# Two attentions rebuilt: heads on halves of a query tile, maxima in paired banks 21 steps ahead, the mask in f32r, row sums inverted inside

## The chip, the core and the metric

The kernel runs on one core of a Trainium2 chip. The metric is the device time of one launch in microseconds (us), the median over the runs shown. The core has TensorE (matrix products into the memory PSUM, eight banks of 512 columns), VectorE, ScalarE, GpSimd and SyncE, which here issues the DMA transfers; each takes its instructions in order and waits on semaphores for the others.

## The reference, cut to what matters

The input x has 2048 rows of 512 columns. The program is a layer of attention plus a gated feed-forward layer, then a gated cumulative sum plus a second attention. The change touches the two attentions:

```python
# attention 0: 32 heads of 16, 8 key heads, causal over N = 2048
scores = einsum('bhqd,bhkd->bhqk', q, k) / sqrt(16)
weight = softmax(where(causal, scores, -inf), axis=-1)
out = einsum('bhqk,bhkd->bhqd', weight, v) @ wo
# attention 1: 16 heads of 32, the same form, causal over 2048
```

All 2048 positions are one sequence in both, so each head has 136 blocks of 128 x 128 on or under the diagonal.

## The kernel before, in words

P is 128, a chunk (CH) is 512 positions, TPC = 4 tiles make a chunk, and there are NCH = 4 chunks and QT = 16 tiles. Products run in f32r with operands split in a high and a low part. For the scores, the parts are stacked along the rows of the array: 3 * DH rows, 48 for attention 0 and 96 for attention 1, and two more rows (96 and 97) carry minus the row maximum, high and low, against ones in k. The rows between are zero in attention 0.

The heads are worked through in 8 groups, of HG = 4 heads in attention 0 and 2 in attention 1. Each group is computed twice. **Maxima** (`max_scores`, L613): TensorE multiplies one query tile i with a chunk kc of keys into a bank of `ps_1` (three banks); VectorE takes the maximum of each row into `mx_part`, with TENSOR_REDUCE (L710) for full blocks, and for blocks at the diagonal with a custom operation that adds `band` first (L706), followed by a short read of the accumulator. When all maxima of 12 tiles (early) or the last 4 (late) are there, `flip` transposes them by a matmul (L624), VectorE splits them in `take_rows` (L727, L729), and SP writes them to memory and reads them into rows 96 and 97 of q (`put_rows`, L534 and L537). **Scores with softmax**: for each chunk c of queries and key tile t (`PASS2_STEPS`, 40 steps a group, 24 full and 16 at the diagonal), TensorE computes two heads into one of two double banks `ps_s` (L663), with a bf16 matmul that adds the mask at the diagonal (L668); ScalarE takes the exponential of both heads at once into `ex` (L596); `times_v` (L635) multiplies the previous step's `ex` with v, whose ones column gives the row sums. Four heads (32 columns each) or two (64) go to column strips of the array and run side by side. At the end of a chunk VectorE copies `ps_o` out (L735) and SP stores it (L544).

The order is written out by hand: in `slot`, each step of group g also does the HG maxima matmuls of the same step of group g + 1, spread between the scores. Before the first group there is an opening with the maxima of all its 40 steps; the last group has none beside it. Three sets of q, k and v rotate; at the start of a group SP loads the set of the group after next (L512 to L521), 2.2 MB in attention 0 and 4 MB in attention 1. `over_slots` loops over three groups by a register. `reciprocals` (L965 to L973) is a block of its own behind each attention: it reads the row sums of all heads from memory, inverts them and writes them to z; `project_out` multiplies with them.

## Time and profile before

| | us |
|---|---|
| median of 3 runs (3016.12 to 3024.72) | 3019.53 |
| the profiled execution | 3012.14 |
| its span, first to last instruction | 3010.3 |
| TensorE busy (matmuls) | 2623.4 (87%) |
| VectorE busy | 1634.4 (54%) |
| ScalarE busy | 1100.0 (37%) |

The times come from one profiled execution. A busy time is the union of an engine's instructions, and matmuls are pipelined: the duration of one counts until its result is out, though the next starts earlier. How long a matmul keeps the array is read from the distance of two starts. [...] "idle before" is how long an engine had nothing to run before a group's instructions, and what ended that.

### The profile page before, as it was taken

The page shows a single profiled execution, that of the slowest core. Times are in us where ns is not written, and L with a number is a line of the kernel's source. Part 1 is how long each engine was busy: PE and PEld are TensorE (multiplying, and loading weights), DVE is VectorE, ACT ScalarE, POOL GpSimd, SP SyncE. Part 2 cuts the span into 40 slices and gives each one's busy share as a digit, 9 for nine tenths or more (in the row PEclk, how much of TensorE's full clock was granted, in tenths as well). Part 3 has the DMA queues.
Part 4 walks back from the last instruction along what each step waited for, and adds up shares of the span by engine and source line. Part 5 has one row for each costly group of instructions (what it writes and reads, how often), then busy time and mean ns, then how long its engine had stood idle before and what let it go on. Part 6 is the DMA issues. An engine that isn't in the chain of part 4 may idle for free. (4 is left out here: it accounts for less than half of the span.)

```text
span 3010.3 us, 38749 instructions
## 1 busy us (share of the span) xinstructions
PE 2623.4 (87%) x12386; PEld 1552.7 (52%) x12386; DVE 1634.4 (54%) x3332; ACT 1100.0 (37%) x1303; POOL 128.9 (4%) x84
## 2 busy tenths in 40 slices
PE   6969999589999999999995799797189999999945
PEld 3758888345555555555543577675144444444314
DVE  4644445587777777777712434311176665666313
ACT  2422222005565555555672222121014444444420
POOL 1200000300000000000000022100300000000000
PEclk8979999659999999999997899898569999999978
DMA  4741010401202202020003100252542122220023
GB/s 157 239 145 42 28 42 0 60 15 28 40 10 42 39 15 42 13 38 10 9 15 132 60 1 0 76 136 102 139 97 55 45 52 72 71 71 12 15 72 120
DMA packets 103924, 177.62 MB, mean 59 GB/s; under 512 B 39664, under 2 KB 45552, under 8 KB 97712
## 3 DMA queue, kind: packets, MB, share of 16 engines
q1 hardware_dynamic: 100272, 162.58, 20.7%
q10 hardware_dynamic: 3456, 12.58, 1.3%
q8 instruction: 104, 1.70, 0.2%
q14 instruction: 92, 0.75, 0.1%
HBM read 115.24 MB, written 59.90 MB: 58 GB/s over the span
## 5 line engine op out<-in xcount | busy, mean ns | idle before, releaser
L596 ACT ACTIVATE a_ex<-a_ps_s 128x1024 f32<-128x1024 f32 x960 | 832.6, 894 | 804.5 <-PE a_ps_s L668 404.1
L710 DVE TENSOR_REDUCE a_mx_part<-a_ps 128x1 f32<-128x512 f32 x1152 | 771.9, 688 | 255.0 <-PE a_ps L613 246.5
L613 PE MATMUL a_ps<-a_k,a_q 96*128 96x512 f32 (+3 forms) x1920 | 786.6, 452 | 97.4 <-DMA a_q<-q 92.8
L613 PEld LDWEIGHTS a_ps<-a_k,a_q 96*128 96x128 f32 x1920 | 369.5, 204 | 586.2 <-DVE a_mx_part L710 326.9
L635 PE MATMUL a_ps_o<-a_ex,a_v 128*32 128x512 f32 (+7 forms) x3840 | 607.6, 548 | 22.8 <-DVE a_o L735 19.1
L663 PE MATMUL a_ps_s<-a_q,a_k 128*128 128x512 f32 (+3 forms) x1920 | 607.6, 392 | 22.3 <-DMA a_q<-m_early 13.7
L706 DVE CUSTOM_DVE_ANT_0 a_junk<-a_ps,band 128x128 f32<-128x128 f32 (+3 forms) x768 | 369.3, 486 | 213.7 <-PE a_ps L613 210.5
L663 PEld LDWEIGHTS a_ps_s<-a_q,a_k 128*128 128x128 f32 x1920 | 353.4, 194 | 119.3 <-ACT a_ex L596 45.4
L635 PEld LDWEIGHTS a_ps_o<-a_ex,a_v 128*32 128x32 f32 (+1 forms) x3840 | 114.2, 117 | 212.9 <-issue 161.0
L668 PE MATMUL a_ps_s<-block_band,block_ident 128*128 128x128 bf16 x768 | 175.0, 234 | 0.0
L110 PE MATMUL w_ps<-w_oh,w_wh 128*128 128x512 f32 x128 | 54.7, 427 | 103.3 <-DVE w_ol L1042 103.3
L668 PEld LDWEIGHTS a_ps_s<-block_band,block_ident 128*128 128x128 bf16 x768 | 75.1, 98 | 84.7 <-issue 53.9
L110 PE MATMUL gc_bank<-xh,gc_wh 128*128 128x512 f32 x256 | 104.0, 406 | 16.3 <-DVE xl L100 16.3
L735 DVE COPY a_o<-a_ps_o 128x512 f32<-128x512 f32 x64 | 43.9, 686 | 135.6 <-PE a_ps_o L635 135.6
L939 DVE TENSOR_TENSOR mlp_hid<-mlp_ps_g,mlp_act_up 128x512 f32<-128x512 f32 x64 | 44.2, 690 | 133.2 <-PE mlp_ps_g L853 124.3
L852 PE MATMUL mlp_ps_u<-xh,mlp_w 128*128 128x512 f32 x256 | 101.2, 395 | 17.0 <-DVE mlp_w L917 17.0
L864 PE MATMUL mlp_ps_y<-mlp_hh,mlp_w 128*128 128x512 f32 x256 | 102.1, 399 | 1.5 <-DVE mlp_hl L942 1.5
L890 ACT ACTIVATE mlp_act_up<-mlp_ps_u,mlp_s 128x512 f32<-128x512 f32 x64 | 44.1, 689 | 159.2 <-PE mlp_ps_u L853 159.2
L111 PE MATMUL gc_bank<-xl,gc_wh 128*128 128x512 f32 x256 | 102.0, 399 | 0.0
L112 PE MATMUL gc_bank<-xh,gc_wl 128*128 128x512 f32 x256 | 102.0, 398 | 0.0
L1370 DVE TENSOR_TENSOR p_ol<-p_bank,p_oh 128x512 fp32r<-128x512 f32 x32 | 22.1, 692 | 145.2 <-ACT p_oh L1331 145.2
L853 PE MATMUL mlp_ps_u<-xl,mlp_w 128*128 128x512 f32 x256 | 100.9, 394 | 0.0
(161 smaller groups left out, 2536.1 us busy)
## 6 DMA issues: line engine op xcount, KB each, us to landing
a_q<-q SPq DMA_DIRECT2D x48, 512.0 KB, 12.3
o<-a_o SPq DMA_DIRECT2D x64, 256.0 KB, 2.4
q<-p_oh SPq DMA_DIRECT2D x32, 256.0 KB
q<-p_ol SPq DMA_DIRECT2D x32, 256.0 KB
w_o<-o SPq DMA_DIRECT2D x32, 256.0 KB
w_z<-z SPq DMA_DIRECT2D x32, 256.0 KB
v<-p_v SPq DMA_DIRECT2D x32, 256.0 KB, 3.4
a_k<-k SPq DMA_DIRECT2D x8, 1024.0 KB, 8.4
```

Source lines behind the costliest of these rows:

```text
L110: pe.matmul(out, wh(k), xh(k), start=k == 0, stop=False)
L111: pe.matmul(out, wh(k), xl(k), start=False, stop=False)
L112: mm = pe.matmul(out, wl(k), xh(k), start=False, stop=k == KT - 1)
L596: act.activation(ex[unit % NE][:, :, off:CH], ps_s[unit % 2][:, :, off:CH], ACT.Exp, scale=SCALE).then_inc(exp_done, 1)
L613: pe.matmul(ps_1[bank][:, 0:w], q_st[set_][0:96, h, i * P:(i + 1) * P], k_st[set_][0:96, h % KH, kc * CH:kc * CH + w], start=True, stop=True)\
L635: mm = pe.matmul(ps_o[h * CT:h * CT + VW, off:CH], v_st[set_][:, h % VH, t, :], ex[(n * PAIRS + h // 2) % NE][:, h % 2, off:CH], start=t = ...
L663: mm = pe.matmul(ps_s[unit % 2][:, h, off:CH], k_st[set_][:, (2 * pair + h) % KH, t * P:(t + 1) * P], q_st[set_][:, 2 * pair + h, c * CH + ...
L668: mm = pe.matmul(ps_s[unit % 2][:, h, off:off + P], block_ident[:, :], block_band[:, :], start=False, stop=True)
L706: dve.tensor_tensor_reduce(out=junk[b][:, 0:w], in0=bank, in1=band[:, CH - w:CH], scale=1.0, scalar=NEG, op0=ALU.add, op1=ALU.max, accum_o ...
L710: dve.tensor_reduce(out, bank, AX.X, ALU.max).then_inc(taken1, 1)
L852: pe.matmul(bank[n % 2][:, :], w[b][i][:, k, cols], xh[:, k, chunk(c)], start=k == 0, stop=False)
L864: pe.matmul(ps_y[:, m, :], w[b][2][:, e, cols], hh[n % 2][:, :], start=e == 0, stop=False)
```

## The change

Both attentions are written anew, with the same mathematics.

- `HALVES` is 2 in attention 0: q holds two heads one above the other, even ones from row 0 and odd ones from row 64 on, and k is loaded twice, into both halves. A score matmul uses 48 (maxima) or 50 rows of one half. The two rows for the maxima stand right behind the operand (row KC), so no rows need to be zero, and q is no longer cleared. Attention 1 has one half (96 and 98 rows).
- Maxima go in blocks of two heads into one of two double banks `ps_1`. VectorE takes full blocks of both heads with one TENSOR_REDUCE; diagonal ones stay one operation per head. They lead the scores by `LEAD` = 21 steps and run on through all groups, without slots. The maxima are transposed per chunk (four times a group), two steps after its last block.
- Scores go head by head into three single banks `ps_s`, with one exponential per head, and `ex` has six buffers for four. ScalarE also copies `ps_o` out.
- The mask is a product in f32r: one matmul per head in attention 1, two of 64 columns in attention 0.
- The row sums are handled inside: after the store of a chunk SP reads the row of sums back (`load_sums`), VectorE inverts it (`invert`), SP stores it (`store_sums`). The block `reciprocals` is gone.
- Loops over registers are gone: the program is written out. The first block of the program, which makes the constants, has more of them to make, by selects one after another, two DMAs and four casts.

```diff
-ATTN0 = dict(HG=4, KH=1, VH=1, DH=16, VW=32, SCALE=16 ** -0.5, GROUPS=8)
-ATTN1 = dict(HG=2, KH=2, VH=2, DH=32, VW=64, SCALE=32 ** -0.5, GROUPS=8)
+ATTN0 = dict(HG=4, KH=1, VH=1, DH=16, VW=32, SCALE=16 ** -0.5, GROUPS=8, HALVES=2)
+ATTN1 = dict(HG=2, KH=2, VH=2, DH=32, VW=64, SCALE=32 ** -0.5, GROUPS=8, HALVES=1)
...
+LEAD = 21
...
+    BLOCKS = [(g, i, kc, p) for g in range(GROUPS) for i in range(QT) for kc in range(i // TPC + 1) for p in range(PAIRS)]
+    LAST_BLOCK = {(g, i // TPC): n for n, (g, i, kc, p) in enumerate(BLOCKS)}
+    FLIP_DELAY = 2 * PAIRS
+    FLIP_AT = {n + 1 + FLIP_DELAY: f for f, n in enumerate(sorted(LAST_BLOCK.values()))}
+    STEP_LIST = [(g, c, t) for g in range(GROUPS) for c, t in PASS2_STEPS]
+    SLOTS = {s: range((s + LEAD) * PAIRS, (s + LEAD + 1) * PAIRS) for s in range(len(STEP_LIST))}
+    SLOTS[-1] = range(0, LEAD * PAIRS)
+    LAST_STEP = {s: (g, c) for s, (g, c, t) in enumerate(STEP_LIST) if t == TPC * c + TPC - 1}
...
-        ps_s = [psum(f"ps_s{i}", [P, 2, CH]) for i in range(2)]
...
+        ps_1 = [psum(f"ps_1{i}", [P, 2, CH]) for i in range(2)]
+        ps_s = [psum(f"ps_s{i}", [P, CH]) for i in range(3)]
...
+                for e in range(HALVES):
+                    r0 = e * ROWS
+                    q_half = q_heads.rearrange("(p e) s r n -> e s r p n", e=HALVES)[e]
+                    sp.dma_start(k_st[s][r0:r0 + 2 * DH].bitcast(F32), k_heads.rearrange("h s r n -> (s r) h n"))\
+                        .then_inc(landed[s], 16)
+                    for r in (0, DH):
+                        sp.dma_start(q_st[s][r0 + r:r0 + r + DH].bitcast(F32), q_half[0]).then_inc(landed[s], 16)
+                    sp.dma_start(k_st[s][r0 + 2 * DH:r0 + KC].bitcast(F32), k_heads[:, 0].rearrange("h r n -> r h n"))\
+                        .then_inc(landed[s], 16)
+                    sp.dma_start(q_st[s][r0 + 2 * DH:r0 + KC].bitcast(F32), q_half[1]).then_inc(landed[s], 16)
...
+            def load_sums(g, c):
+                j = g * NCH + c
+                b = j % 2
+                sp.wait_ge(stored[b], 16 * (j // 2 + 1))
+                if j >= 2:
+                    sp.wait_ge(inverse, j - 1)
+                src = o_d[g].rearrange("(h r) (c m n) -> c r h m n", h=HG, c=NCH, n=ZN)[c, CT // 2]
+                sp.dma_start(z[b][:, :], src).then_inc(z_in[b], 16)
...
+            for s in range(-1, len(STEP_LIST) + 8):
+                for n in SLOTS.get(s, ()):
+                    if n in FLIP_AT:
+                        put_rows(FLIP_AT[n], n)
+                if s >= 0 and s < len(STEP_LIST) and s % STEPS == 2 and s // STEPS + 2 < GROUPS:
+                    if s // STEPS > 0:
+                        sp.wait_ge(pv_done, s // STEPS * STEPS)
+                    elif ONES0 < KC:
+                        sp.wait_ge(blank, 3)
+                    load(s // STEPS + 2)
+                if s - 2 in LAST_STEP:
+                    store(*LAST_STEP[s - 2])
+                if s - 3 in LAST_STEP:
+                    load_sums(*LAST_STEP[s - 3])
+                if s - 6 in LAST_STEP:
+                    store_sums(*LAST_STEP[s - 6])
...
+            for s, (g, c, t) in enumerate(STEP_LIST):
+                if s - 2 in LAST_STEP:
+                    stage(*LAST_STEP[s - 2], s - 2)
+                off = first_col(c, t)
+                for h in range(HG):
+                    n = s * HG + h
+                    unit = s * PAIRS + h // 2
+                    act.wait_ge(scores2, n + 1)
+                    if h % 2 == 0 and unit >= NE:
+                        act.wait_ge(pv_done, (unit - NE) // PAIRS + 1)
+                    act.activation(ex[unit % NE][:, h % 2, off:CH], ps_s[n % 3][:, off:CH], ACT.Exp, scale=SCALE)\
+                        .then_inc(exp_done, 1)
...
+            def max_scores(n):
+                g, i, kc, p = BLOCKS[n]
+                s = g % NS
+                m = entry(n)
                 w = min(CH, (i + 1) * P - kc * CH)
...
+                if (i, kc, p) == (0, 0, 0):
+                    pe.wait_ge(landed[s], LOADS * (g // NS + 1))
+                if m >= 2:
+                    pe.wait_ge(taken1, m - 1)
+                for e in (1, 0):
+                    h = 2 * p + e
+                    r0, slot_h = h % HALVES * ROWS, h // HALVES
+                    mm = pe.matmul(ps_1[m % 2][:, e, 0:w], q_st[s][r0:r0 + KC, slot_h, i * P:(i + 1) * P],
+                                   k_st[s][r0:r0 + KC, h % KH, kc * CH:kc * CH + w], start=True, stop=True)
+                mm.then_inc(scores1, 1)
...
+            def scores(s, h):
+                g, c, t = STEP_LIST[s]
+                n, st = s * HG + h, g % NS
                 off = first_col(c, t)
...
+                r0, slot_h = h % HALVES * ROWS, h // HALVES
+                if n >= 3:
+                    pe.wait_ge(exp_done, n - 2)
+                diagonal = t >= TPC * c
+                mm = pe.matmul(ps_s[n % 3][:, off:CH], k_st[st][r0:r0 + KM, h % KH, t * P:(t + 1) * P],
+                               q_st[st][r0:r0 + KM, slot_h, c * CH + off:(c + 1) * CH], start=True, stop=not diagonal)
+                for part in range(HALVES if diagonal else 0):
+                    sel, low = mask
+                    cols = slice(off + part * ROWS, off + (part + 1) * ROWS)
+                    r0 = h % HALVES * ROWS
+                    mm = pe.matmul(ps_s[n % 3][:, cols], sel[r0:r0 + ROWS, part, :], low[r0:r0 + ROWS, :],
+                                   start=False, stop=part == HALVES - 1)
+                mm.then_inc(scores2, 1)
...
+            for s, (g, c, t) in enumerate(STEP_LIST):
+                if t == 0:
+                    f = g * NCH + c
+                    pe.wait_ge(rows_in[f % 2], ROWS_IN * (f // 2 + 1))
+                for p in range(PAIRS):
+                    n = SLOTS[s][p]
+                    scores(s, 2 * p)
+                    if n in FLIP_AT:
+                        flip(n)
+                    if n < len(BLOCKS):
+                        max_scores(n)
+                    scores(s, 2 * p + 1)
+                if s > 0:
+                    times_v(s - 1)
...
+                if kc < i // TPC:
+                    dve.tensor_reduce(mx_part[:, 2 * p:2 * p + 2, i, kc], bank[:, :, 0:w], AX.X, ALU.max)\
+                        .then_inc(taken1, 1)
+                    return
+                for e in range(2):
+                    last = dve.tensor_tensor_reduce(out=junk[m % 2][:, e, 0:w], in0=bank[:, e, 0:w], in1=band[:, CH - w:CH],
+                                                    scale=1.0, scalar=NEG, op0=ALU.add, op1=ALU.max,
+                                                    accum_out=mx_part[:, 2 * p + e, i, kc:kc + 1])
+                last.then_inc(taken1, 1)
...
+            def invert(g, c):
+                j = g * NCH + c
+                dve.wait_ge(z_in[j % 2], 16 * (j // 2 + 1))
+                if j >= 2:
+                    dve.wait_ge(z_out[j % 2], 16 * (j // 2))
+                dve.reciprocal(zr[j % 2][:, :], z[j % 2][:, :]).then_inc(inverse, 1)
+            for s in range(-1, len(STEP_LIST) + 8):
+                for n in SLOTS.get(s, ()):
+                    if n in FLIP_AT:
+                        take_rows(n)
+                    if n < len(BLOCKS):
+                        maxima(n)
+                        g, i, kc, p = BLOCKS[n]
+                        if LAST_BLOCK[g, i // TPC] == n:
+                            whole_max(g, i // TPC, n)
+                if s - 5 in LAST_STEP:
+                    invert(*LAST_STEP[s - 5])
...
-def reciprocals(nc, keep, sems, name, heads, rows, o_d, z_d):
...
-        block_ident, block_band = sb("block_ident", [P, P], BF16), sb("block_band", [P, P], BF16)
...
+        masks = {1: (sb("mask_sel1", [P, 1, P], F32R), sb("mask_low1", [P, P], F32R)),
+                 2: (sb("mask_sel2", [P, 2, P], F32R), sb("mask_low2", [P, P // 2], F32R))}
...
```

How the instructions move is shown at two places. The first is TensorE in attention 0 in a step with full blocks (L613 and L612 are the maxima, L663 and L633 the scores, L635 and L651 the product with v). Before:

```order
L661 REGISTER_ALU
L663 MATMUL a_ps_s<-a_q,a_k 128x512 [waits attn_exp_done]
L663 MATMUL a_ps_s<-a_q,a_k 128x512
L612 REGISTER_ALU
L613 MATMUL a_ps<-a_k,a_q 128x512 [waits attn_taken1]
L661 REGISTER_ALU
L663 MATMUL a_ps_s<-a_q,a_k 128x512 [waits attn_exp_done]
L663 MATMUL a_ps_s<-a_q,a_k 128x512
L612 REGISTER_ALU
L613 MATMUL a_ps<-a_k,a_q 128x384 [waits attn_taken1]
L635 MATMUL a_ps_o<-a_ex,a_v 32x512 [waits attn_exp_done]
L635 MATMUL a_ps_o<-a_ex,a_v 32x512 x3
```

and now:

```order
L633 MATMUL a_ps_s<-a_q,a_k 128x512 [waits at_exp_done]
L612 MATMUL a_ps<-a_k,a_q 128x512 [waits at_taken1]
L612 MATMUL a_ps<-a_k,a_q 128x512
L633 MATMUL a_ps_s<-a_q,a_k 128x512 [waits at_exp_done] x2
L612 MATMUL a_ps<-a_k,a_q 128x512 [waits at_taken1]
L612 MATMUL a_ps<-a_k,a_q 128x512
L633 MATMUL a_ps_s<-a_q,a_k 128x512 [waits at_exp_done]
L651 MATMUL a_ps_o<-a_ex,a_v 32x512 [waits at_exp_done]
L651 MATMUL a_ps_o<-a_ex,a_v 32x512 x3
```

The numbers of columns stay, eight score matmuls between two products; the pairs of maxima wait once, the scores each for a bank of their own, and successive matmuls are in opposite halves of the array.

The second is the start of a group, steps 1 to 5, on SP in attention 0 (L522 stores the last chunk of the group before, L494 to L501 load a later group, L532 reads the row sums, L509 and L514 move the maxima):

```order
L522 DMA o<-a_o 128x512 [waits at_staged]
L494 DMA a_k<-k 32x2048 [waits at_pv_done]
L497 DMA a_q<-q 16x2x2048 x2
L498 DMA a_k<-k 16x2048
L500 DMA a_q<-q 16x2x2048
L494 DMA a_k<-k 32x2048
L497 DMA a_q<-q 16x2x2048 x2
L498 DMA a_k<-k 16x2048
L500 DMA a_q<-q 16x2x2048
L501 DMA a_v<-v 128x512
L532 DMA a_z<-o 128x1x16 [waits at_inverse,at_stored1]
L509 DMA m<-a_rows_0 16x128 [waits at_taken1]
L509 DMA m<-a_rows_1 16x128
L514 DMA a_q<-m 2x2x512 [waits at_rows_out0]
```

The read of the row sums is issued behind all loads of a group; before, only the rows of maxima were there. On VectorE the inversion of them (L724) stands between the maxima (L690 and L694):

```order
L690 TENSOR_REDUCE a_mx_part<-a_ps 128x2 [waits at_scores1] x4
L724 RECIPROCAL a_zr<-a_z 128x16 [waits at_z_in0]
L690 TENSOR_REDUCE a_mx_part<-a_ps 128x2 [waits at_scores1] x2
L694 ISA a_junk,a_mx_part<-a_ps,band 128x256 [waits at_scores1]
L694 ISA a_mx_part 128x1
L694 ISA a_junk,a_mx_part<-a_ps,band 128x256
L694 ISA a_mx_part 128x1
L694 ISA a_junk,a_mx_part<-a_ps,band 128x256 [waits at_scores1]
```

Before, no instruction of VectorE in an attention waited for the row sums.

## Rows read from the trace of the kernel before

**Rows 1.** Busy time by stretch: us; PE, PEld, DVE, ACT, POOL busy (instructions); PEclk; DMA share, GB/s

```profile
574.50:672.90 98.40, 88.28 (x163) 45.08 (x163) 87.79 (x228) 0.00 (x0) 0.75 (x1) 0.50 0.19 25
680.00:1514.00 834.00, 824.40 (x4950) 437.66 (x4950) 648.25 (x1628) 480.00 (x561) 0.00 (x0) 0.99 0.15 26
1514.00:1598.00 84.00, 81.71 (x532) 33.54 (x530) 3.32 (x6) 64.97 (x78) 0.00 (x0) 1.00 0.03 11
2174.50:2233.30 58.80, 47.67 (x93) 24.64 (x93) 44.88 (x120) 1.20 (x2) 10.06 (x3) 0.50 0.40 90
2233.30:2822.60 589.30, 569.00 (x2492) 246.71 (x2491) 364.15 (x850) 251.28 (x282) 0.00 (x0) 0.99 0.22 55
2822.60:2885.00 62.40, 61.13 (x266) 21.91 (x266) 3.19 (x6) 34.62 (x39) 0.00 (x0) 1.00 0.05 18
```

**Rows 2.** Timeline of TensorE over one step: start us, us, engine, line, what, count

```profile
1139.26 1.07 PE L635 MATMUL a_ps_o<-a_ex,a_v 128*32 128x512 f32 x8
1140.26 0.68 PE L613 MATMUL a_ps<-a_k,a_q 96*128 96x512 f32 x2
1140.77 0.64 PE L663 MATMUL a_ps_s<-a_q,a_k 128*128 128x512 f32 x2
...
1141.48 0.63 PE L663 MATMUL a_ps_s<-a_q,a_k 128*128 128x512 f32 x2
1141.94 0.40 PE L613 MATMUL a_ps<-a_k,a_q 96*128 96x512 f32 x1
1142.27 0.64 PE L635 MATMUL a_ps_o<-a_ex,a_v 128*32 128x512 f32 x4
```

**Rows 3.** VectorE: group in 680:1514, timeline, the tile w_z, group of the page

```profile
L710 DVE TENSOR_REDUCE a_mx_part<-a_ps 128x1 f32<-128x512 f32 x672 | 448.8, 687 | 141.1 <-PE a_ps L613 138.0 <-issue 1.1
...
1139.13 1.29 DVE L710 TENSOR_REDUCE a_mx_part<-a_ps 128x1 f32<-128x512 f32 x2
...
L1040 DVE TENSOR_TENSOR w_o<-w_o,w_z x8: 2284/2291/2293, 1626.3 to 2984.3; 128x2048 f32<-128x2048 f32 x8
...
L706 DVE CUSTOM_DVE_ANT_0 a_junk<-a_ps,band 128x128 f32<-128x128 f32 (+3 forms) x768 | 369.3, 486 | 213.7 <-PE a_ps L613 210.5
```

**Rows 4.** ScalarE: timeline in the last group of attention 0, groups in 680:1514

```profile
1547.70 1.94 ACT L596 ACTIVATE a_ex<-a_ps_s 128x1024 f32<-128x1024 f32 x2 [0.18 <-PE a_ps_s L663]
...
L596 ACT ACTIVATE a_ex<-a_ps_s 128x1024 f32<-128x1024 f32 x392 | 380.0, 1021 | 219.8 <-PE a_ps_s L663 179.7 <-PE a_ps_s L668 39.8
...
L596 ACT ACTIVATE a_ex<-a_ps_s 128x512 f32<-128x512 f32 x56 | 33.4, 597 | 50.9 <-PE a_ps_s L668 49.5
```

**Rows 5.** Timeline of VectorE at the attentions' ends and start

```profile
545.35 6.88 DVE L692 MEMSET a_q<- 128x8192 f32 x1 [2.15 <-issue]
...
1604.24 3.35 DVE L973 RECIPROCAL r_zr<-r_z 128x512 f32<-128x512 f32 x1 [6.34 <-DMA r_z<-o]
...
2890.31 1.75 DVE L973 RECIPROCAL r_zr<-r_z 128x256 f32<-128x256 f32 x1 [5.18 <-DMA r_z<-o]
```

**Rows 6.** Timeline of SP's DMA issues at two group starts; the page's DMA issues

```profile
1159.26 0.33 SPq L512 DMA_DIRECT2D a_k<-k  x1
...
1163.49 0.79 SPq L534 DMA_DIRECT2D m_late<-a_rows_late  x2
1179.52 0.64 SPq L537 DMA_DIRECT2D a_q<-m_late  x1
...
2318.07 0.73 SPq L512 DMA_DIRECT2D a_k<-k  x1
...
2339.47 0.68 SPq L537 DMA_DIRECT2D a_q<-m_late  x1
...
o<-a_o SPq DMA_DIRECT2D x64, 256.0 KB, 2.4
```

**Rows 7.** Busy time by stretch and TensorE's timeline behind the loop's turn

```profile
1034.00:1040.00 6.00, 5.67 (x20) 3.74 (x20) 1.56 (x10) 3.98 (x4) 0.00 (x0) 0.54 0.90 152
...
1040.72 1.94 PE L635 MATMUL a_ps_o<-a_ex,a_v 128*32 128x512 f32 x8
```

More of the change, by code:

```diff
@@ L482, in attention @@
-        block = ctx.enter_context(nc.Block())
-        def first_col(c, t):
-            return max(0, t - TPC * c) * P
-        def bank1(entry, first=False):
-            if entry >= NB or first:
-                return entry % NB if not first else (entry + ENTRIES) % NB, entry - NB
-            return entry, max(e for e in range(ENTRIES) if e % NB == entry) - ENTRIES
-        def over_slots(eng, slot):
-            turns = (GROUPS - 2) // 3
-            with eng.Fori(0, turns) as turn:
-                for s in range(3):
-                    slot(turn, s)
-            for s in range(2):
-                slot(turns, s, last=s == 1, loads=False)
+        z_in = [sem(f"z_in{i}") for i in range(2)]
@@ L553, in slot @@
-            def slot(turn, s, last=False, loads=True):
-                g, set_ = turn * 3 + s, s % 3
-                if loads:
-                    sp.wait_ge(pv_done, g * STEPS + PV0)
-                    sp.sem_inc(sp_passed, 1)
-                    load(turn, s + 2, (s + 2) % 3)
-                put_rows(g, set_, False, g * ENTRIES + (FIRST + (0 if last else FLIP_LATE * HG)))
-                for c in range(NCH - 1):
-                    store(g, c)
-                if not last:
-                    put_rows(g + 1, (s + 1) % 3, True, g * ENTRIES + (FIRST + (FLIP_EARLY + 1) * HG + 1))
-                store(g, NCH - 1)
@@ L689, in _ @@
+            times_v(len(STEP_LIST) - 1)
         @block.vector
         def _(dve):
[L691 to L692 removed]
             dve.memset(mx_part[:, :, :, :], NEG).then_inc(part_init, 1)
             dve.wait_ge(part_init, 1)
[L696 to L710 removed]
@@ L1281, in _ @@
         def _(sp):
-            for s in used.values():
+            for s in reused.values():
                 sp.sem_clear(s)
```

456 lines of the change are left out of this document (177 added, 279 removed).

## The prediction, made before the changed kernel ran

> **What bounds the kernel now.** I first read the busy times by stage [rows 1]. The two attentions take most of the program. Attention 0 computes maxima alone for 98.4 us, then runs seven groups with the next group's maxima mixed in, 834 us or 119 a group, and ends with a group without maxima, 84 us. Attention 1 has the same three parts: 58.8, 589.3 (84.2 a group) and 62.4 us. In both mixed parts TensorE is busy for over 96% of the time, VectorE for 78% and 62%. A busy TensorE need not be full, so the second view is TensorE's timeline over one full step of attention 0 [rows 2]. The product with v lasts 1.00 us (1139.26 to 1140.26), two maxima matmuls behind it 0.51, then scores and maxima follow each other every 0.23 to 0.24, and 0.33 lies between the last of them and the next product: 3.01 us, hardly a gap. The third view is VectorE's groups [rows 3]: in the mixed part it is idle for 141.1 us before full-width reductions, 138.0 of it waiting for TensorE. So TensorE bounds both mixed parts; in the opening it is VectorE (87.79 of 98.4 us, with TensorE's clock at 0.50).
>
> **Attention 0, TensorE.** With 48 or 50 of 128 rows used, the change puts two heads in the two 64-row halves of the array and orders the matmuls low, high, low, high. No row of this trace shows row halves running at once, but column strips do: the eight matmuls of a v product take 1.07 us together. Bounds: a pair of halves costs the place of one matmul (0.235) or of two (0.47). I take one, since the v product is the nearest row. A full step is then 4 x 0.235, plus 0.10 for going over to the v product (0.33 less 0.235), plus 1.00: 2.04 us, against 3.01.
> [...]
>
> **Attention 0, VectorE.** A reduction of 512 columns begins 1.29 - 0.69 = 0.60 us after the one before. An operation on 2048 columns takes 2.29, so a column costs (2.29 - 0.69) / 1536 = 1.04 ns, and a paired reduction of 1024 should cost 0.60 + 0.53 = 1.13. A step with full blocks needs 2 x 1.13 = 2.27 us, more than TensorE's 2.04: **VectorE becomes the bound**. Diagonal blocks stay four operations, (0.486 - 0.09) x 4 = 1.6 on average, 0.8 to 2.4 by width.
> ScalarE is third: 0.92 for two heads, less 1.021 - 0.597 for 512 columns, is 0.495 for one [rows 4], so 1.98 a step. The copies of the output that it takes over, 4 x 0.5 a group, hide in its slack.
> With two double banks there is also a loop: from a freed bank over TensorE to the refill of the other one. A load of weights about 0.1, pair 0.24, score 0.24, going over 0.10, v product 1.00, the next pair behind a score 0.24, its 0.40 until the result, a signal 0.05: 2.4 us. I take **2.4 for the 24 full-block steps**, 2.2 for 12 of the diagonal ones, 2.43 for the 4 widest, and 3 us for the four transposes of maxima (they were two): 57.6 + 26.4 + 9.7 + 3 = 97 us a group, against 119.
> The diagonal mask becomes two f32r matmuls of 64 columns per head with weights of their own. No row prices those; the bounds are nothing and a place of 0.235 each, up to 1.9 us on 16 short steps. I take 0.2 to 0.4, under the 2.2, as short matmuls lie beside the other half's.
>
> **Attention 0 in all.** The opening has 21 block-steps instead of 40, 10 full (22.7) and 11 diagonal (17.1): 40 us. Then 299 of the 320 steps carry maxima: 299 x 97 / 40 = 725. The last 21 run at ScalarE's 2.1: 44. That is 809 us for 1023 (rows 1, from 574.5 to 1598): **-214**.
>
> **Attention 1** keeps whole columns of the array (98 rows), so its matmuls do not overlap. Its f32r mask costs between nothing and 32 x 0.235 = 7.5 a group; I take 1.5, with a little less waiting at paired banks: 85.5 us for 84.2. Opening 26, 299 x 85.5 / 40 = 639, last 21 steps at 1.7 = 36: 701 for 710, **-9**.
>
> **Small terms.** The first block gains a chain of selects, a DMA (2.4) and casts: +5. The loads of attention 0 no longer stand behind the 6.88 us in which q is cleared: -7. The reciprocals of 3.35 and 1.75 us leave the path with a barrier each [rows 5]: -7.
>
> **The wait that is added.** The row sums are now inverted inside: SP stores o, reads the sums row back (z), VectorE inverts it five steps after the chunk's end, and all later maxima stand behind that wait in its queue. For chunk 3 of groups 0 to 4, the order puts z's small load right behind the loads of a whole later group. What happens to a small transfer there the trace shows: the rows issued at 1163.49 let SP go on at 1179.52, 20.3 us after the load began at 1159.26; in attention 1 it is 21.4 us. Without a load a store lands in 2.4 us [rows 6]. Attention 0 now loads 2.5 MB for 2.2, so I take 23 us. The load starts some 1.5 us into step 1 of a group, so z lands 25 us after that step began. VectorE comes to the wait after step 4 and TensorE, with both banks full, stops 10.6 us after step 1 began (4 x 2.4 + 1): a stall of 15 us, five times = 74. In attention 1 it is 1.5 + 21.4 less 10 = 13, five times = 65. Bounds: 0 and 20 each. Behind such a gap TensorE starts at the low clock: behind the turn of the loop the trace has 0.54 and a v product of 1.94 us, for 1.07 [rows 7]. I add 1.8 us each, ten times = 18. The rows of maxima that are stuck in the same loads are covered by this stall.
>
> **Sum.** 5 - 7 - 214 + 74 + 9 - 9 + 65 + 9 - 7 = -75. The profiled execution took 3012.1, so 2937; the median of the three runs is 7.4 above it, which gives **2945 us**. The likeliest case's own range is 2880 to 3005.
>
> **Rivals.**
> *z passes the load, or the stall is hidden* (0.14). For it: z is only 8 KB. Against it: the 16 us of the rows at 1163.49. It gives 2937 - 157 + 7, about 2790.
> *The row halves do not run at once* (0.13), the rival on the slower side. TensorE keeps its step of 3.01 and pays for twice the masks: about 121 us a group, 299 x 121 / 40 + 40 + 50 = 994 instead of 809, and the stalls stay: 3130. It decides once a pair costs over 0.32 (4 x 0.32 + 1.10 = 2.4), and past about 0.39 (75 us over 299 x 4 places is 0.06) the kernel is slower than before.
> [...]
> *The clock stays low in attention 0* (0.04), since TensorE would idle for 15% of a step: in the openings it ran at 0.50 though busy for 90%. A step is then 1.87 + 4 x 0.46 + 0.1 = 3.8 us, 299 x 1.4 more: 3360. Against it, TensorE at that clock would be full again.
> *The change does little*: halves that overlap in part. Within 0.3% of the median (0.04) or near it on either side (0.07).
>
> **Chances.** My forecast has 0.58. A measurement of this kernel can tell about 0.3%, 9 us, from no change. Faster: 0.58 + 0.14 + 0.05 = 0.77; same 0.04; slower 0.13 + 0.04 + 0.02 = 0.19. The range, 2780 to 3060, takes in the first rival and leaves out 3130 and 3360, 0.17, and little else.
>
> **What would show it.** Score matmuls starting in pairs far less than 0.23 us apart; VectorE some 90% busy in attention 0 outside the stalls; full steps of 2.3 to 2.5 us; an opening of 40. For the added wait: five gaps in each attention of 13 to 15 us, ended on VectorE by z's landing, the clock low behind them, and z 20 us on its way there but about 2.5 elsewhere. It is wrong if full steps still take 3 us, if no reciprocal waits for over 5 us, or if attention 1's groups outside the stalls leave 82 to 89 us.

## The result, and the profile after the change

The changed kernel takes **3065.9 us** (median of 4 runs, 3053.1 to 3077.5), the kernel before 3021.2 (4 runs, 3016.1 to 3024.7): the ratio is 1.0148, with a 95% interval of 1.0105 to 1.0192. It is slower, by 1.5%. The forecast was 2945, in a range of 2780 to 3060, and faster. Times are medians, and of the ten runs of e2_v_between below one, 3069 us in a slower state of the chip, is left out. The profiled execution took 3077.5 (span 3075.7), the slowest of the four; my sum for it was 2937, so it is off by 140.

Busy time by stretch of the changed kernel, with the columns of [rows 1] (us; PE, PEld, DVE, ACT, POOL busy; PEclk, the clock granted to TensorE as a share of the full one; DMA share, GB/s). The three stretches of each attention are its opening, the part with maxima, and the rest:

```profile
575.00:623.80 48.80, 35.03 (x120) 17.68 (x120) 46.13 (x117) 3.62 (x7) 0.00 (x0) 0.50 0.68 91
623.80:1561.00 937.20, 863.12 (x5870) 433.49 (x5869) 650.85 (x1417) 581.91 (x1243) 0.00 (x0) 0.84 0.14 26
1561.00:1622.00 61.00, 57.91 (x220) 20.84 (x220) 0.25 (x1) 30.29 (x64) 0.00 (x0) 0.50 0.02 5
2192.70:2222.40 29.70, 24.57 (x58) 14.67 (x58) 23.69 (x62) 1.62 (x3) 0.00 (x0) 0.50 0.81 180
2222.40:2888.00 665.60, 602.20 (x2558) 285.37 (x2558) 334.84 (x738) 309.94 (x597) 0.00 (x0) 0.92 0.20 48
2888.00:2951.00 63.00, 61.94 (x267) 25.37 (x265) 17.41 (x33) 36.24 (x73) 0.00 (x0) 1.00 0.05 14
```

Against [rows 1], each opening is halved (98 to 49 us, 59 to 30; 40 and 26 were forecast). But the part with maxima in attention 0 has lost TensorE's clock: 0.84 on the mean for 0.99, and the rest stands at 0.50 throughout, for 1.00. From the first maxima matmul to the last v product attention 0 takes 1046 us (before 1022), attention 1 758 (before 706).

TensorE's timeline of a full step of attention 0 at the full clock, and of one at the low clock:

```profile
1184.78 0.50 PE L633 MATMUL a_ps_s<-a_q,a_k 50*128 50x512 f32 x1
1184.79 0.44 PE L612 MATMUL a_ps<-a_k,a_q 48*128 48x384 f32 x1
1185.07 0.39 PE L633 MATMUL a_ps_s<-a_q,a_k 50*128 50x512 f32 x1
...
1185.30 0.39 PE L633 MATMUL a_ps_s<-a_q,a_k 50*128 50x512 f32 x1
...
1185.97 0.50 PE L633 MATMUL a_ps_s<-a_q,a_k 50*128 50x512 f32 x1
1186.40 1.07 PE L651 MATMUL a_ps_o<-a_ex,a_v 128*32 128x512 f32 x8
1187.39 0.50 PE L633 MATMUL a_ps_s<-a_q,a_k 50*128 50x512 f32 x1
...
1223.05 0.79 PE L633 MATMUL a_ps_s<-a_q,a_k 50*128 50x512 f32 x1
...
1224.53 0.79 PE L633 MATMUL a_ps_s<-a_q,a_k 50*128 50x512 f32 x1
1225.25 1.94 PE L651 MATMUL a_ps_o<-a_ex,a_v 128*32 128x512 f32 x8
1227.12 0.79 PE L633 MATMUL a_ps_s<-a_q,a_k 50*128 50x512 f32 x1
```

A score and a maxima matmul of the two halves start within 0.01 us of each other, so the halves do run at once. The step takes 2.61 us (1184.78 to 1187.39): three scores go 0.23 to 0.29 apart, and the fourth only 0.67 behind the third. The same step at the low clock takes 4.07.

The stop for the row sums, in group 4, by VectorE's and TensorE's timelines:

```profile
1158.92 0.25 DVE L724 RECIPROCAL a_zr<-a_z 128x16 f32<-128x16 f32 x1 [11.29 <-DMA a_z<-o]
...
1159.67 0.80 PE L612 MATMUL a_ps<-a_k,a_q 48*128 48x512 f32 x2 [11.05 <-DVE a_rows L716]
1160.27 0.62 PE L633 MATMUL a_ps_s<-a_q,a_k 50*128 50x512 f32 x1
1160.82 1.93 PE L651 MATMUL a_ps_o<-a_ex,a_v 128*32 128x512 f32 x8
```

VectorE's group of reciprocals over the whole program (busy, mean ns, then idle before):

```profile
L724 DVE RECIPROCAL a_zr<-a_z 128x16 f32<-128x16 f32 (+1 forms) x64 | 14.1, 221 | 239.0 <-DMA a_z<-o 239.0
```

The read of the sums had been issued at 1143.12, right behind the eleven transfers of a load that began at 1137.91; it lets VectorE go on 15.8 us later, 21.0 us after the load began. The five stops of attention 0 are 10.9 to 12.4 us, 57 in all, the five of attention 1 are 14.0 to 14.8, 72 in all. The rest of the 239 us lies near the attentions' ends, where little or no maxima work is left to hold up.

### The profile page after: what moved, and what is told of

Its sections match the earlier page's. It is cut to its first block and busy times, and to the rows that moved or that the text cites. A ratio compares the mean times of both kernels' runs of the same rounds, so it can differ in the third digit from the quotient of the medians.

```text
span 3075.7 us, 34326 instructions
## 1 busy us (share of the span) xinstructions
PE 2594.9 (84%) x12962; PEld 1540.2 (50%) x12962; DVE 1539.9 (50%) x2851; ACT 1229.1 (40%) x2325; POOL 99.1 (3%) x83
## 5 line engine op out<-in xcount | busy, mean ns | idle before, releaser
L593 ACT ACTIVATE a_ex<-a_ps_s 128x512 f32<-128x512 f32 (+3 forms) x1920 | 937.8, 536 | 883.6 <-PE a_ps_s L633 465.4
L612 PE MATMUL a_ps<-a_k,a_q 48*128 48x512 f32 (+6 forms) x1920 | 639.5, 464 | 235.8 <-DVE a_rows L716 119.5
L690 DVE TENSOR_REDUCE a_mx_part<-a_ps 128x2 f32<-128x1024 f32 x576 | 684.8, 1221 | 284.5 <-PE a_ps L612 281.4
L633 PE MATMUL a_ps_s<-a_q,a_k 50*128 50x512 f32 (+7 forms) x1920 | 764.0, 455 | 7.3 <-ACT a_ex L593 5.1
L651 PE MATMUL a_ps_o<-a_ex,a_v 128*32 128x512 f32 (+7 forms) x3840 | 678.3, 619 | 0.5 <-ACT a_o L581 0.5
L633 PEld LDWEIGHTS a_ps_s<-a_q,a_k 50*128 50x128 f32 (+1 forms) x1920 | 363.4, 207 | 590.1 <-ACT a_ex L593 410.1
L612 PEld LDWEIGHTS a_ps<-a_k,a_q 48*128 48x128 f32 (+1 forms) x1920 | 328.6, 213 | 318.3 <-DVE a_rows L716 130.8
L694 DVE CUSTOM_DVE_ANT_0 a_junk<-a_ps,band 128x128 f32<-128x128 f32 (+3 forms) x768 | 337.1, 486 | 202.4 <-PE a_ps L612 199.8
L639 PEld LDWEIGHTS a_ps_s<-mask_low,mask_sel 64*128 64x128 f32 (+1 forms) x1280 | 218.4, 205 | 9.1
L639 PE MATMUL a_ps_s<-mask_low,mask_sel 64*128 64x64 f32 (+1 forms) x1280 | 217.9, 250 | 0.0
L651 PEld LDWEIGHTS a_ps_o<-a_ex,a_v 128*32 128x32 f32 (+1 forms) x3840 | 119.0, 123 | 157.9 <-ACT a_ex L593 110.8
L724 DVE RECIPROCAL a_zr<-a_z 128x16 f32<-128x16 f32 (+1 forms) x64 | 14.1, 221 | 239.0 <-DMA a_z<-o 239.0
L110 PE MATMUL gc_bank<-xh,gc_wh 128*128 128x512 f32 x256 | 104.6, 409 | 16.3 <-DVE xl L100 16.3
L823 PE MATMUL mlp_ps_g<-xh,mlp_w 128*128 128x512 f32 x256 | 100.3, 392 | 0.0
## 6 DMA issues: line engine op xcount, KB each, us to landing
a_q<-q SPq DMA_DIRECT2D x48, 256.0 KB, 12.4
```

The source lines that it names most:

```text
L110: pe.matmul(out, wh(k), xh(k), start=k == 0, stop=False)
L593: act.activation(ex[unit % NE][:, h % 2, off:CH], ps_s[n % 3][:, off:CH], ACT.Exp, scale=SCALE)\
L612: mm = pe.matmul(ps_1[m % 2][:, e, 0:w], q_st[s][r0:r0 + KC, slot_h, i * P:(i + 1) * P], k_st[s][r0:r0 + KC, h % KH, kc * CH:kc * CH + w], ...
L633: mm = pe.matmul(ps_s[n % 3][:, off:CH], k_st[st][r0:r0 + KM, h % KH, t * P:(t + 1) * P], q_st[st][r0:r0 + KM, slot_h, c * CH + off:(c + 1 ...
L639: mm = pe.matmul(ps_s[n % 3][:, cols], sel[r0:r0 + ROWS, part, :], low[r0:r0 + ROWS, :], start=False, stop=part == HALVES - 1)
L651: mm = pe.matmul(ps_o[h * CT:h * CT + VW, off:CH], v_st[g % NS][:, h % VH, t, :], ex[(s * PAIRS + h // 2) % NE][:, h % 2, off:CH], start=t ...
```

## The experiments

Three theories stood at the start. **B**: three score banks bind the step. **Z**: the row sums behind the loads stop the kernel. **C**: the clock is lost, which I had priced at 1.8 us for each stop. What the low clock hangs on was open: in the expectations "Z+C" has the stops as its cause, and "theory C" of e4_whole_tile the half-empty array. Att 0 and att 1 are read from each profile, from the first maxima matmul to the last v product; "low" is the time in att 0 at a clock of 0.50. The expectations of e1_load_late and e3_both call the two levels of the clock 1.2 and 2.4 GHz; the profiles show it as a share alone, 0.50 and 1.00.

| kernel | us | ratio to before (95%) | att 0 | low | att 1 |
|---|---|---|---|---|---|
| before | 3021 | | 1022 | 118 | 706 |
| changed | 3066 | 1.011 to 1.019 | 1046 | 410 | 758 |
| e1_load_late | 2898 | 0.956 to 0.962 | 967 | 300 | 665 |
| e2_v_between | 3037 | 1.001 to 1.008 | 1042 | 471 | 740 |
| e3_both | 2926 | 0.965 to 0.971 | 999 | 362 | 666 |
| e4_whole_tile | 3935 | 1.298 to 1.308 | 1916 | 1916 | 739 |
| e5_whole_98 | 3071 | 1.013 to 1.019 | 1042 | 128 | 751 |
| e6_filled | 2847 | 0.939 to 0.945 | 903 | 122 | 666 |
| e7_four_banks | 2937 | 0.969 to 0.977 | 977 | 299 | 663 |
| e8_four_filled | 2840 | 0.936 to 0.943 | 893 | 53 | 664 |
| e9_tail_banks | 2818 | 0.930 to 0.935 | 873 | 66 | 665 |
| e10_twice_first | 2977 | 0.983 to 0.991 | 1023 | 160 | 669 |
| e11_twice_last | 2861 | 0.943 to 0.950 | 912 | 124 | 668 |
| e12_filled_only | 3001 | 0.991 to 0.997 | 981 | 227 | 739 |

The first column and the others are not from the same executions: a profile is one run, and the kernels that lose the clock most spread widest (e12_filled_only 2978 to 3022, e7_four_banks 2909 to 2944 with the fastest of them profiled, but e6_filled 2846 to 2849). Attention 1 has the same code in the changed kernel, e2_v_between, e4_whole_tile, e5_whole_98 and e12_filled_only, and took 739 to 758 in their profiles; a difference of less than some 20 us between two kernels with stops says little.

### The load moved

```diff
-                if s >= 0 and s < len(STEP_LIST) and s % STEPS == 2 and s // STEPS + 2 < GROUPS:
+                if s >= 0 and s < len(STEP_LIST) and s % STEPS == 27 and s // STEPS + 2 < GROUPS:
```

> One number changed in the changed kernel: the load of the group after next is issued at step 27 of a group instead of step 2, where no row sums are on their way for 12 steps. Theory Z+C (the row sums stuck behind a load stop the kernel ten times for 12 to 13 us, and each stop also leaves TensorE at 1.2 GHz for 20 to 48 us afterwards): no reciprocal waits over 3 us, the ten stops go (-125), and the low-clock steps behind them go too (some 267 us in attention 0 at 4.07 instead of 2.61 a step, -96; 86 us in attention 1, -40): about 2805. Theory Z alone (the clock falls because the array is underfilled, whatever the stops): -125, about 2940, low-clock time as before. Rival (the wait only moves: rows of maxima or something else then stand behind the load): over 3000. The full step at full clock stays 2.61 in every theory, and the tail of attention 0 stays at 4.07 a step.

Measured: 2898, 168 below the changed kernel, where 129 us of stops and their aftermath were at stake. The expectation takes the low stretches of 20 to 48 us as following the stops; they include them. In the changed kernel the clock came back 10 to 36 us after the five stops of attention 0. All ten stops are gone now (what is left of waits for the sums, 110 us, lies at the attentions' ends). Attention 1 is settled by this alone. Its part with maxima by stretch:

```profile
2140.00:2776.00 636.00, 635.27 (x2825) 300.06 (x2823) 353.61 (x770) 345.40 (x668) 0.00 (x0) 1.00 0.22 54
```

TensorE is busy for all of it at the full clock, 80.7 us a group. Attention 0 is not settled: it is still at 0.50 for 300 us of 967, so 2898 and not the 2805 of Z+C. Theory Z holds; the stops were not all of the clock's story.

### The v product between the pairs

```diff
                     scores(s, 2 * p + 1)
+                    if DEEP and p == 0 and s > 1:
+                        times_v(s - 2)
-                if s > 0:
+                if not DEEP and s > 0:
                     times_v(s - 1)
```

> The loads stay at step 2. In attention 0 the product with v of step s-2 is placed between the two pairs of scores of step s, instead of that of step s-1 behind them (the copy of the output, the inversion and the store of the sums come one to two steps later to match). Theory B (three single score banks for four heads, with the v product between the last score and the next first one, bind a full step to 2.61 us: 0.53 + 0.65 + 0.43 + 1.00): the full step falls to VectorE's 2.27 to 2.35, 7 us a group, -55; if the clock is lost through gaps in TensorE's work, the low-clock stretches shorten as well and the last 21 steps of attention 0 run at 2.1 to 2.4 instead of 4.07 a step, another -45 to -90: 2920 to 2965 in all. Rival (VectorE or the row halves bind the step): 2.6 stays, 3050 to 3080. The ten stops for the row sums stay in every theory, perhaps shorter by one step.

> Both edits: loads at step 27, and in attention 0 the v product of step s-2 between the pairs. If banks, row sums and clock are the three causes and their terms add: 2680 to 2740, attention 0 at 2.3 a full step and over 95% of it at 2.4 GHz, below both of the single edits by what the other gave. If the clock is lost by an underfilled array in any case, attention 0 shows low stretches still and the time is 2780 or more.

Both missed what theory B forecast: 3037 is 29 below the changed kernel and lies between the two ranges, 2926 is 28 above e1_load_late. Both spend more time at the low clock than the same kernel without this edit (471 for 410, 362 for 300). Of the 25 us by which e2_v_between's profile is the shorter one (3052 to 3077), 18 lie in attention 1, where its code is the same; in attention 0 shorter stops (VectorE's five waits for the sums are 23 us, for 57) make up for the low time. The full step did not move, as TensorE's timeline of e2_v_between shows:

```profile
957.63 1.07 PE L652 MATMUL a_ps_o<-a_ex,a_v 128*32 128x512 f32 x8
958.63 0.50 PE L634 MATMUL a_ps_s<-a_q,a_k 50*128 50x512 f32 x1
...
958.92 0.40 PE L634 MATMUL a_ps_s<-a_q,a_k 50*128 50x512 f32 x1
...
959.15 0.39 PE L634 MATMUL a_ps_s<-a_q,a_k 50*128 50x512 f32 x1
959.15 0.62 PE L613 MATMUL a_ps<-a_k,a_q 48*128 48x512 f32 x2
959.82 0.50 PE L634 MATMUL a_ps_s<-a_q,a_k 50*128 50x512 f32 x1
960.25 0.64 PE L652 MATMUL a_ps_o<-a_ex,a_v 128*32 128x512 f32 x4
```

Wherever the v product stands, four scores lie between it and the next, and there are three banks: the fourth score (959.82) waits for the exponential of the first (958.63), 1.19 us later. My cure was wrong; whether the bind was right too, these two runs leave open. The two exponentials below settle it.

### Whole tile, with 50 rows and with 98

```diff
-ATTN0 = dict(HG=4, KH=1, VH=1, DH=16, VW=32, SCALE=16 ** -0.5, GROUPS=8, HALVES=2)
+ATTN0 = dict(HG=4, KH=1, VH=1, DH=16, VW=32, SCALE=16 ** -0.5, GROUPS=8, HALVES=1)
```

and, for e5_whole_98 on top of it (besides the clearing of q and k):

```diff
-    KM = KC + 2
+    KL = 96 if DH == 16 else KC
+    KM = KL + 2
...
-                    mm = pe.matmul(ps_1[m % 2][:, e, 0:w], q_st[s][r0:r0 + KC, slot_h, i * P:(i + 1) * P],
+                    mm = pe.matmul(ps_1[m % 2][:, e, 0:w], q_st[s][r0:r0 + KL, slot_h, i * P:(i + 1) * P],
```

> The changed kernel with HALVES = 1 in attention 0: every head on the whole query tile, so that no two score or maxima matmuls run side by side; paired maxima banks, single score banks and the row sums inside stay. Full step at full clock: eight places of 0.235 + 0.10 + 1.00 = 2.98 against 2.61, so +0.37 on 299 steps = +110. Theory C (a half-empty array is what lets the clock go): the steps are full again, the low-clock time in attention 0 falls from 412 to some 150 us and gives back 90 to 110: about 3065 to 3090, granted clock of attention 0 over 0.9. Theory Z+C (stops are what lets the clock go): low-clock time much as now, 3130 to 3180. If it is at or below the changed kernel's time, the halves bring nothing as built.

The first of them, e4_whole_tile, came out 750 us beyond either theory, at 3935. Both had let the clock follow the gaps in TensorE's work, and here it has none: busy time by stretch (columns as above):

```profile
640.00:1500.00 860.00, 860.00 (x2598) 432.87 (x2594) 333.83 (x705) 311.03 (x599) 0.00 (x0) 0.50 0.08 14
```

and one row of its timeline, with the maxima's shape (rows of the array * columns of weights):

```profile
1055.27 1.05 PE L612 MATMUL a_ps<-a_k,a_q 48*128 48x512 f32 x2
```

TensorE is busy for 860.00 of 860 us, and its clock stays at 0.50. If busy time as the profile shows it were what counts, this kernel would have the best clock of all; the measurement decides against it. What differs from the kernel before is in the shape: 48 and 50 rows of the array, where that one fed 96 and 128 [rows 2] at a clock of 0.99 [rows 1]. So a new theory **R**: the clock follows how much of the array the matmuls use, zeros or not.

> As e4_whole_tile (every head of attention 0 on the whole query tile), but laid out as in the kernel before: rows 48 to 95 of q and k are cleared, the maxima and ones stand in rows 96 and 97, so a score matmul uses 98 rows and a maxima matmul 96, half of them zeros; result and instruction order are the same, three clearing operations of some 7 us each are added ahead. Theory R (TensorE's clock in attention 0 follows how many rows of the array the matmuls use, zeros or not: 50 rows left it at 0.50 for all 1916 us although TensorE had no gap): the clock comes back to over 0.9, full steps from 5.57 to 3.0 to 3.1, attention 0 from 1916 to some 1080, the kernel 3080 to 3180. Rival (the clock is low through the order of matmuls, the single banks or the waits of the new structure, not the rows): still 3850 to 3950.

Measured: 3071, 863 us less, by filling the operands with zeros (9 us under the range expected). The same stretch of e5_whole_98:

```profile
640.00:1500.00 860.00, 815.96 (x4842) 471.89 (x4841) 602.59 (x1317) 543.23 (x1119) 0.00 (x0) 0.96 0.14 24
```

The clock is back at 0.96 with TensorE busy for less of the time, and the full step is 3.07 for 5.57. R holds: with the same order of matmuls, the same banks and the same waits, the rows in use decide here: 0.50 with 48 and 50, 0.96 with 96 and 98. The rows that the change saved, by no longer clearing q and feeding 96 to 128 rows, are what held the clock up here.

### The halves filled

e6_filled is e1_load_late with the idea of e5_whole_98 for two halves: rows 48 to 61 of each are filled (zeros in q, ones in k), `KL` is 62. e12_filled_only is that without the moved load.

```diff
+    KL = 62 if DH == 16 else KC
+    KM = KL + 2
...
+                for e in range(HALVES if KL > KC else 0):
+                    pool.memset(q_st[s][e * ROWS + 32:e * ROWS + 64].bitcast(F32), 0.0)
```

> As e1_load_late, and in attention 0 each half is filled up: rows 48 to 61 are zeros in q and ones in k, the maxima stand in rows 62 and 63, so a maxima matmul uses 62 rows for 48 and a score matmul 64 for 50; the values are the same. Theory R (rows in use hold the clock): the 300 us at 0.50 of attention 0 fall to under 150, most of all in the last 21 steps, and each takes some 0.35 of its time along: 2898 - 55 = 2840, down to 2800. Rival (gaps in TensorE's work alone let the clock go): 2898 plus 4 for clearing, the low time as in e1_load_late within 40 us.

> The changed kernel with the halves of attention 0 filled up to 64 rows and nothing else; the loads are at step 2 again. Terms that add: attention 0 as in e6_filled (903) plus five stops of 12.5 and five stretches of 14 us at the low clock behind them (5 each, as in e5_whole_98), some 990; attention 1 as in the changed kernel (758): 3066 - 56 = 3010, between 2995 and 3020. If the low clock of the changed kernel comes from the stops rather than from the rows in use, 3050 or more; if filling carries the clock over the stops, 2985 or less.

Measured: 2847 (forecast 2800 to 2840, so 7 above) and 3001 (2995 to 3020). Of the low time, 49 us are the opening and 61 the last steps in each of these kernels. The rest is 300 us in the changed kernel (some 50 of it inside the stops), 190 with the load moved, 117 with the rows filled, 12 with both. So neither alone keeps the clock: with 48 and 50 rows a side it falls at the stops, stays low for 10 to 36 us after them, and falls in groups without a stop. By stretch, e6_filled from its first v product to the end of the maxima, and from there to the last v product:

```profile
626.80:1419.00 792.20, 768.58 (x5860) 393.98 (x5859) 648.40 (x1417) 574.52 (x1241) 0.00 (x0) 0.99 0.19 33
1419.00:1480.60 61.60, 58.62 (x225) 21.18 (x229) 0.25 (x1) 31.31 (x65) 0.00 (x0) 0.50 0.02 5
```

A group now takes 104.3 us against 117.9 in the kernel before. The last steps, where I had expected the filling to help most, are still at the low clock.

### Four score banks

e7_four_banks is e1_load_late with one bank moved from the maxima to the scores, so that the maxima of each head are reduced apart; e8_four_filled has the filled halves of e6_filled as well.

```diff
+        ps_1 = [psum(f"ps_1{i}", [P, CH]) for i in range(3)]
+        ps_s = [psum(f"ps_s{i}", [P, CH]) for i in range(4)]
...
+                if n >= 4:
+                    pe.wait_ge(exp_done, n - 3)
```

> As e1_load_late, with four single banks for the scores instead of three and three single banks for the maxima instead of two double ones, so each head's maxima of a full block are reduced apart, as in the kernel before. The run with the v product between the pairs left the full step at 2.61, and its timeline shows why: with three banks one of the four scores between two v products always waits for the exponential of the first behind the last product, wherever the product stands. Theory B (that wait binds the step): now nothing waits for a score bank and VectorE binds, four reductions at 0.60 make 2.4 to 2.45 instead of 2.61 on the 24 full steps a group, -32 to -40, and TensorE has no gap of 0.4 any more: 2810 to 2865. Rival V (VectorE's unpaired reductions with three banks cost as much as the wait did): full step 2.6 or more, 2890 to 2950.

> e6_filled and e7_four_banks together. If both of their theories hold the gains add: 2750 to 2820, with attention 0 over 0.93 in granted clock. If only the banks matter it equals e7_four_banks within 10 us plus 4 for clearing; if only the rows, e6_filled.

Measured: 2937 and 2840. The first is in the range of rival V; the second missed 2750 to 2820 and is near e6_filled. Rival V holds for the full step, but by its banks: 2.74 us instead of 2.61. TensorE's timeline of e8_four_filled has the wait:

```profile
990.28 0.49 PE L637 MATMUL a_ps_s<-a_q,a_k 64*128 64x512 f32 x1
...
991.59 0.50 PE L616 MATMUL a_ps<-a_k,a_q 62*128 62x512 f32 x1 [0.34 <-DVE a_mx_part L696]
991.59 0.50 PE L637 MATMUL a_ps_s<-a_q,a_k 64*128 64x512 f32 x1
```

The bank moved from scores to maxima, and the fourth maxima matmul waits for VectorE. Groups get longer (107.6 for 104.3), yet the kernel is 7 us shorter (2840 for 2847), within the noise of both. The cause is the last group, 91 us for 122: with four score banks and no maxima left, its last steps take 1.96 to 2.12 us at a clock of 1.00. That gave the next edit.

### Seven banks for the last steps

e9_tail_banks is e6_filled with the scores from step 303 of 320 on (`TAIL`) in seven banks, the three of the scores and the four that the maxima no longer need.

```diff
+        TAIL = 4 * 303 if PAIRS == 2 else HG * len(STEP_LIST)
+        spare = [ps_1[i][:, j, :] for i in range(2) for j in range(2)]
+
+        def score_bank(n):
+            return (ps_s + spare)[(n - TAIL) % 7] if n >= TAIL else ps_s[n % 3]
```

> As e6_filled, and in attention 0 the scores of the last 17 steps, when the maxima are done, rotate through seven banks: the three score banks and the four of the maxima. In e6_filled these steps take 4.07 us each at 0.50; with four score banks (e8_four_filled) they take 1.96 to 2.12 at full clock. Theory B+R (waits for a bank leave gaps that let the clock go, and at the low clock the same wait is longer): 17 x 2.0 = -33, the kernel at 2810 to 2818. Rival (without maxima the work is too thin for the full clock, whatever the banks; e8_four_filled differed in other things): 3.3 to 4.0 us a step, 2833 to 2850.

Measured: 2818.1 (6 runs, 2813.0 to 2821.9), ratio to before 0.9327 (0.930 to 0.935). It is the fastest kernel of the study, ahead of both the kernel before and the changed one. The last steps of e6_filled and of this kernel, by TensorE's timelines:

```profile
1442.94 1.93 PE L654 MATMUL a_ps_o<-a_ex,a_v 128*32 128x512 f32 x8
...
1446.29 0.79 PE L636 MATMUL a_ps_s<-a_q,a_k 64*128 64x512 f32 x1 [0.26 <-ACT a_ex L596]
1447.01 1.94 PE L654 MATMUL a_ps_o<-a_ex,a_v 128*32 128x512 f32 x8
```

```profile
1429.18 1.06 PE L664 MATMUL a_ps_o<-a_ex,a_v 128*32 128x512 f32 x8 [0.23 <-ACT a_ex L602]
1430.18 0.50 PE L646 MATMUL a_ps<-a_q,a_k 64*128 64x512 f32 x1
1430.18 0.73 PE L646 MATMUL a_ps_s<-a_q,a_k 64*128 64x512 f32 x3
1431.14 1.06 PE L664 MATMUL a_ps_o<-a_ex,a_v 128*32 128x512 f32 x8 [0.23 <-ACT a_ex L602]
```

1.96 us a step instead of 4.07, at a clock of 1.00 instead of 0.50, though TensorE waits 0.23 us for ScalarE in each. So without the three-bank wait the clock stays. But that wait alone does not lose it. e5_whole_98 has the same three banks, and its last steps by TensorE's timeline and by stretch (columns as above) are:

```profile
1590.58 1.07 PE L659 MATMUL a_ps_o<-a_ex,a_v 128*32 128x512 f32 x8
...
1592.76 0.49 PE L641 MATMUL a_ps_s<-a_q,a_k 98*128 98x512 f32 x1 [0.22 <-ACT a_ex L601]
1593.18 1.06 PE L659 MATMUL a_ps_o<-a_ex,a_v 128*32 128x512 f32 x8
```

```profile
1584.80:1621.00 36.20, 33.80 (x189) 13.65 (x193) 0.25 (x1) 27.95 (x59) 0.00 (x0) 1.00 0.03 8
```

Its step is 2.60 us, the loop of theory B, at a clock of 1.00. It took both to lose the clock in the last steps: the wait, and matmuls on 64 rows instead of 98. From step 303 to the end e6_filled takes 61 us, e5_whole_98 39 and e9_tail_banks 30, so about 22 of the 31 us between e6_filled and e9_tail_banks are the clock, and the other 9 the bank wait at the full clock.

### One exponential twice

Both runs are e6_filled with one more exponential in each step of attention 0.

```diff
+                    if PAIRS == 2 and h == 0:
+                        act.activation(spare[s % 2][:, off:CH], ps_s[n % 3][:, off:CH], ACT.Exp, scale=SCALE)
                     act.activation(ex[unit % NE][:, h % 2, off:CH], ps_s[n % 3][:, off:CH], ACT.Exp, scale=SCALE)\
```

(`h == 3` in e11_twice_last.)

> As e6_filled, with the exponential of the first head of each step of attention 0 computed twice (once more, into a spare buffer, ahead of the one that frees the bank), which gives ScalarE 0.48 us more a step, 2.47 in all. Theory B (the step is the loop v product, first score, its exponential, fourth score, v product): the first exponential lies on the loop, so a full step goes from 2.61 to 3.09, and 200 or more of the 320 steps with it: +95 to +120, 2940 to 2970. Rival S (ScalarE has slack of 0.63 a step and TensorE or VectorE binds): within 15 us of e6_filled.

> The same extra work on ScalarE, but for the fourth head of each step: its exponential is off the loop of theory B, and ScalarE is idle for 0.54 us before the next first one. Theory B: full step 2.61 to 2.70, the kernel within 20 us of e6_filled (2847 to 2867), some 90 below e10_twice_first. If ScalarE's total were what counts, both of these kernels would take the same time.

Measured: 2977 (7 above its range) and 2861 (as expected), so +131 and +14 for the same added work. A full step with the first exponential twice, by TensorE's timeline:

```profile
1003.11 1.07 PE L657 MATMUL a_ps_o<-a_ex,a_v 128*32 128x512 f32 x8
1004.11 0.50 PE L639 MATMUL a_ps_s<-a_q,a_k 64*128 64x512 f32 x1
...
1005.78 0.50 PE L639 MATMUL a_ps_s<-a_q,a_k 64*128 64x512 f32 x1 [0.48 <-ACT a_ex L599]
1006.21 1.07 PE L657 MATMUL a_ps_o<-a_ex,a_v 128*32 128x512 f32 x8
```

The step is 3.10 for 2.61: all of the 0.48 lies on it. The fourth score now waits 1.67 us behind the first, 1.19 before. Theory B is shown: v product 1.00, first score to its exponential 0.53, exponential and signal 0.65, fourth score to the next v product 0.43. VectorE, at 2.27, and ScalarE's total were not the bound.

## Why the prediction was wrong, point by point

Attention 0 took 1046 us where I had 892 (809 + 74 + 9), and attention 1 758 for 775; the rest of the program is off by 3. The 154 of attention 0 split by the runs, which take its parts away one at a time:

- **The row halves**: right. Pairs start together and keep 0.23 us of place. My rival of 3130, halves that do not run at once, was wrong. Groups without a stop or a low clock take 104.3 us with the halves (e6_filled) and 117.0 on the whole tile (e5_whole_98, its group before the last), so the halves are worth 12.7 us a group.
- **"VectorE becomes the bound", 2.4 for a full step, 97 us a group**: wrong bound, undersized. The paired reduction costs 1.13, as worked out, but I looked for a loop only through the maxima's double banks. The one through the three score banks gives 2.61, and a group 104.3: 7.3 x 299 / 40 = 55 us.
- **The opening**: 49 for 40, +9. It runs at 0.50 and VectorE binds it (46.13 of 48.80).
- **The stop behind the loads**: right in kind, place and count; 57 for 74 in attention 0, 72 for 65 in attention 1. The sums let VectorE go on 21.0 us after the load began, where I had 23, and with steps of 2.61 instead of 2.4 it came to the wait later.
- **"I add 1.8 us each, ten times = 18"**: this is the step that failed. In attention 0 I had 9 us for the clock. It cost some 108: 65 through the rows in use (e12_filled_only to changed, in attention 0), about 22 in the last steps (of the 30 from e6_filled to e9_tail_banks, 8 are the bank wait at the full clock), 21 behind the stops even with rows filled (981 less 903 and 57). I saw 0.50 behind a gap [rows 7] and took the 0.99 of the kernel before [rows 1] as given. The change cut the rows that matmuls use from 96 and 128 to 48 and 50, two of them side by side where a partner is there, and put waits into each step. I gave "the clock stays low in attention 0" 0.04 and argued that a full TensorE would hold its clock; e4_whole_tile shows a full one that does not (860.00 of 860 us busy, at 0.50).
- **The last 21 steps of attention 0 at 2.1, 44 us**: 30 more, the 22 and the 8 above, since the last 61 us ran at 0.50 and waited for a third bank; with banks to spare the 44 came (873 = 49 + 104.3 x 299 / 40 + 44 in e9_tail_banks).

That is 55 + 9 - 17 + 108 + 8 - 9 = 154. It splits one profile of each kernel, and the changed kernel's was the slowest of its four, 12 us over the median, so the parts are good to some 10 us at best.

- **Attention 1**: 36 us better than forecast without stops (665 for 701; a group 80.7 for 85.5, and 84.2 in the kernel before, so the f32r mask cost nothing that shows; what made the group shorter was not tried apart), then 72 for the stops and 21, not 9, for the clock behind them. In e2_v_between, e4_whole_tile and e12_filled_only, with the same code there, those 21 are 2 or 3, and in e5_whole_98 14.

With the clock at the 18 us that I gave it, the sum would have come to 3077 - 99 - 12 = 2966, inside my range. That 3066 lies only 6 us above that range is luck: attention 1's groups and the stops gave back 46 us of what the clock and the step had taken. Three small choices, the step of the load, the row count of a half and the banks of the last steps, lie between 3066 and 2818.

## What to carry to other kernels

Before a change that narrows the operands of a matmul, ask what holds the clock now: zero rows that look like waste may pay for themselves, and the test is cheap: here they were worth 52 to 65 us with halves, 863 on a whole tile. Count the banks against the operations between two long ones on the same engine; here the surplus one, the fourth score, waited for a whole chain, 1.19 us behind the first, wherever the long one was put. And issue a bulk load where no small transfer is due behind it, since here the small one landed with the load: 15.8 us after its issue, where the last transfer of a load takes 16.3 (median).
